# Keys of two attention layers laid in blocks of two heads, and their score products split into two halves of 32 rows

## The reference

```
q = rms_norm(x @ Wq + bq, gq).reshape(b, -1, n, d)
k_img = rms_norm(ctx_img @ Wk_img + bk_img, gk_img).reshape(b, -1, n, d)
v_img = (ctx_img @ Wv_img + bv_img).reshape(b, -1, n, d)
img_x = _attend(q, k_img, v_img)
out = (txt_x + img_x).reshape(b, -1, n * d)
return out @ Wo + bo
```

## Time and profile before

| | |
|---|---|
| Median of three runs | 3621.99 us (3617.33 to 3624.5) |
| The profiled execution | 3609.43 us, span 3607.7 us |
| Scatter stage with the keys and values | about 670 to 902 us of the span |
| Attention of layer 2 | about 2003 to 2205 us |
| Attention of layer 3 | about 2615 to 2816 us |

### The profile page before, as it was taken

One profiled execution on the slowest core, in us unless ns is written; L12 is line 12 of the kernel. 1 busy time (PEld: TensorE's weight loads), 2 busy tenths in 40 slices (PEclk: granted clock), 3 DMA queues, 4 the chain that ended last, 5 costly groups with the idle time before them and its releaser, 6 DMA issues. The chain is left out here.

```text
span 3607.7 us, 60300 instructions
## 1 busy us (share of the span) xinstructions
PE 2864.7 (79%) x20178; PEld 1832.3 (51%) x20178; DVE 2156.4 (60%) x4946; ACT 1479.5 (41%) x3032; POOL 1108.2 (31%) x1494
## 2 busy tenths in 40 slices
PE   5488886366899994589847798999889649999993
PEld 4233334122455553433323585444478648888882
DVE  7699994677677775634578686888777610000003
ACT  5377773254222224589835453222255211111120
POOL 3211110377233335412298441000044431111110
PEclk7599996698999997599969899999999669999996
DMA  8766643499422223688300440000044221112104
GB/s 272 195 114 119 120 105 140 151 371 356 138 80 82 77 82 132 166 136 137 59 1 1 160 145 27 1 1 1 1 160 133 96 60 56 47 53 79 60 29 140
DMA packets 261417, 386.10 MB, mean 107 GB/s; under 512 B 56673, under 2 KB 188750, under 8 KB 260864
## 3 DMA queue, kind: packets, MB, share of 16 engines
q1 hardware_dynamic: 230288, 305.68, 31.6%
q0 software_dynamic: 25152, 68.22, 5.4%
q10 hardware_dynamic: 5680, 8.39, 0.7%
HBM read 227.49 MB, written 160.24 MB: 107 GB/s over the span
## 5 line engine op out<-in xcount | busy, mean ns | idle before, releaser
L3172 POOL DMA_INDIRECT rows_out<-e_out,e_tr_dest x224 | 234.8, 1048 | 867.3 <-DVE e_out L3822 506.4
L3822 DVE COPY e_out<-e_psD 128x512 f32<-128x512 f32 x40 | 27.7, 692 | 495.4 <-PE e_psD L3790 495.2
L1243 ACT ACTIVATE a_pt<-a_psS 128x512 f32<-128x512 f32 x512 | 277.6, 595 | 107.9 <-PE a_psS L1139 103.5
L3584 PE MATMUL e_psG<-e_wgu,e_yT 128*128 x576 | 277.8, 605 | 29.3 <-ACT e_yT L3616 26.7
L1265 DVE TENSOR_REDUCE a_mx_sb<-a_psM 128x4 f32<-128x1024 f32 x256 | 293.2, 1215 | 12.3 <-PE a_psM L1122 11.4
L1153 PE MATMUL a_psV<-a_pt,a_vt 128*18 128x256 f32 x4096 | 291.2, 386 | 2.6 <-issue 2.1
L3790 PE MATMUL e_psD<-e_w,e_hT 128*128 128x256 f32 x1280 | 291.8, 388 | 0.0
L3779 PE MATMUL e_psH<-e_yT,e_w 128*128 128x256 f32 x1280 | 284.5, 381 | 1.6 <-issue 0.8
L3722 ACT ACTIVATE e_hT<-e_psH 128x512 f32<-128x512 f32 x160 | 95.5, 597 | 454.0 <-PE e_psH L3779 454.0
L3790 PEld LDWEIGHTS e_psD<-e_w,e_hT 128*128 128x128 f32 x1280 | 247.2, 196 | 33.7
L3779 PEld LDWEIGHTS e_psH<-e_yT,e_w 128*128 128x128 f32 x1280 | 244.2, 191 | 35.6 <-issue 2.1
(11 more groups left out here) (433 smaller groups left out, 6126.0 us busy)
## 6 DMA issues: line engine op xcount, KB each, us to landing
kbd<-e_wd SPq DMA_DIRECT2D x64, 512.0 KB, 3.8
cr_kbd<-kbd SPq DMA_DIRECT2D x64, 512.0 KB, 3.6
rows_in<-zeros POOLq DMA_DIRECT2D x36, 522.0 KB, 6.5
e_xin<-rows_in SPq DMA_DIRECT2D x144, 128.0 KB
vbd<-e_bd SPq DMA_DIRECT2D x64, 272.0 KB, 3.9
cr_vbd<-vbd SPq DMA_DIRECT2D x64, 272.0 KB, 2.7
cq_rows<-rows_out SPq DMA_DIRECT2D x32, 512.0 KB, 6.0
e_w<-in_L_ffn_w_dram SPq DMA_DIRECT2D x16, 1024.0 KB, 7.6
```

What stands on the lines that cost most here:

```text
L1243: act.activation(pt[:, probs(t, h), b, :, :], psS[:, unit(t, h, b) % S_BANKS, :].rearrange("p (k c) -> p k c", k=KC), ACT.Exp, scale=scale ...
L3172: pool.indirect_dma_start(out=self.rows_out[0:limit, :], out_offset=bass.IndirectOffsetOnAxis(ap=self.dest[:, t:t + 1], axis=0), in_=rows, ...
L3584: ins = pe.matmul(psG[:, u, :], yT[:, u, k, :], wgu[:, e, k, :], start=(k == 0), stop=(k == KC - 1))
```

## The change

CJ becomes 2. The keys are laid in blocks of two heads: 32 partitions with 128 columns, so an item is 128 partitions by 512 columns, 256 KB, in SBUF, in the store and in the load. The mask for it is cut in four parts of 32 partitions. A tile's scores become 16 products of 32 rows and 128 columns, in two halves j of eight: half 0 on the row groups 0 and 1, half 1 on the row groups 2 and 3. Both halves write to the same two PSUM banks, and the second waits for the last products of the first. In TensorE's step the first half stands where the scores stood, then come the turn of the input and the query projection, then the second half, then the turn of the probabilities. Semaphores of the scores become four.

```
-CJ = 4
+CJ = 2
+CR = CJ * CW
...
-        self.kbd = room_a[:, 12:16, :].rearrange("p (u x) c -> p u (x c)", u=2)
+        self.kbd = room_a[:, 12:14, :]
...
-        for half in range(2):
-            rows = self.mask[SEQ * half:SEQ * half + SEQ, :]
+        pool.wait_ge(self.made, 6)
+        for part in range(P // CR):
+            rows = self.mask[CR * part:CR * part + CR, :]
...
-    s_done = [core.sem(f"{n}sd{r}") for r in range(2)]
+    s_done = [core.sem(f"{n}sd{g}") for g in range(2 * CJ)]
...
-                def scores(t):
+                def scores(t, j):
                     u, m = t % 3, t % NK
-                    pe.wait_ge(q_ready, t + 1)
-                    pe.wait_ge(k_loaded[m], 16 * (t // NK + 1))
-                    if t:
-                        pe.wait_ge(shifted, t)
+                    if j == 0:
+                        pe.wait_ge(q_ready, t + 1)
+                        pe.wait_ge(k_loaded[m], 16 * (t // NK + 1))
+                        if t:
+                            pe.wait_ge(shifted, t)
+                    else:
+                        for r in range(2):
+                            pe.wait_ge(s_done[r], t + 1)
                     for k in range(KC):
                         for b in range(2):
                             for r in range(2):
-                                rows = slice(SEQ * r, SEQ * r + SEQ)
-                                ins = pe.matmul(psS[SEQ * b:SEQ * b + SEQ, r, k, :], qT[rows, u, k, SEQ * b:SEQ * b + SEQ],
-                                                kbd[rows, m, k, b, :], start=True, stop=True, tile_position=(SEQ * r, SEQ * b))
+                                g = 2 * j + r
+                                rows = slice(CR * g, CR * g + CR)
+                                ins = pe.matmul(psS[SEQ * b:SEQ * b + SEQ, r, k, j, :], qT[rows, u, k, SEQ * b:SEQ * b + SEQ],
+                                                kbd[rows, m, k, b, :], start=True, stop=True, tile_position=(CR * g, SEQ * b))
...
                     if ok(s + 1):
-                        scores(s + 1)
+                        scores(s + 1, 0)
                     if ok(s + 4):
                         turn_y(s + 4)
-                    if ok(s):
-                        turn_probs(s)
                     if ok(s + 3):
                         project(s + 3)
+                    elif ok(s):
+                        turn_probs(s)
+                    if ok(s + 1):
+                        scores(s + 1, 1)
+                    if ok(s) and ok(s + 3):
+                        turn_probs(s)
                     if ok(s - 1):
                         values(s - 1)
...
-                        for r in range(2):
-                            dve.wait_ge(s_done[r], t + 1)
+                        for g in range(2 * CJ):
+                            dve.wait_ge(s_done[g], t + 1)
```

More of the change, by code:

```diff
@@ L1452, in gpsimd_setup @@
                 pool.memset(v[SEQ * hh:SEQ * hh + SEQ, :, hh, CW], 1.0).then_inc(self.made, 1)
-        for half in range(2):
-            rows = self.mask[SEQ * half:SEQ * half + SEQ, :]
+        pool.wait_ge(self.made, 6)
+        for part in range(P // CR):
+            rows = self.mask[CR * part:CR * part + CR, :]
             pool.affine_select(out=rows, in_=rows, compare_op=ALU.is_ge, fill=0.0, base=0,
                                pattern=[[-CW, CJ]], channel_multiplier=1).then_inc(self.made, 1)
-        pool.wait_ge(self.made, 8)
-        for half in range(2):
-            rows = self.mask[SEQ * half:SEQ * half + SEQ, :]
+        pool.wait_ge(self.made, 10)
+        for part in range(P // CR):
+            rows = self.mask[CR * part:CR * part + CR, :]
             pool.affine_select(out=rows, in_=rows, compare_op=ALU.is_ge, fill=0.0, base=CW - 1,
                                pattern=[[CW, CJ]], channel_multiplier=-1).then_inc(self.made, 1)
-        pool.wait_ge(self.made, 10)
+        pool.wait_ge(self.made, 14)
     def gpsimd(self, pool, tile):
@@ L1503, in square @@
             act.activation(self.junk, self.kv[:, i % 4, 0:DIM], ACT.Square, accum_out=self.square[:, i:i + 1]).then_inc(self.squared, 1)
-        act.wait_ge(self.made, 10)
+        act.wait_ge(self.made, 14)
         for i in range(self.ITEMS):
@@ L1522, in vector_setup @@
         dve.tensor_tensor(self.gain, self.gain, self.query_gain, ALU.mult).then_inc(self.gained, 1)
-        dve.wait_ge(self.made, 10)
+        dve.wait_ge(self.made, 14)
         dve.wait_ge(self.gained, 1)
@@ L1622, in phase_cross @@
         psQ = ps(ctx, n + "psQ", [P, 2, DIM])
-        psS = ps(ctx, n + "psS", [P, 2, KC, CJ * SEQ])
+        psS = ps(ctx, n + "psS", [P, 2, KC, 2, CJ * SEQ])
         psP = ps(ctx, n + "psP", [P, 2, 4, P])
@@ L1647, in _ @@
                     if t >= NK:
-                        for r in range(2):
-                            sp.wait_ge(s_done[r], t - NK + 1)
+                        for g in range(2 * CJ):
+                            sp.wait_ge(s_done[g], t - NK + 1)
                     sp.dma_start(kbd[:, t % NK, :, :, :].rearrange("p k b c -> p (k b c)"), kbd_dram[t]).then_inc(k_loaded[t % NK], 16)
@@ L1732, in scores @@
                             for r in range(2):
-                                rows = slice(SEQ * r, SEQ * r + SEQ)
-                                ins = pe.matmul(psS[SEQ * b:SEQ * b + SEQ, r, k, :], qT[rows, u, k, SEQ * b:SEQ * b + SEQ],
-                                                kbd[rows, m, k, b, :], start=True, stop=True, tile_position=(SEQ * r, SEQ * b))
+                                g = 2 * j + r
+                                rows = slice(CR * g, CR * g + CR)
+                                ins = pe.matmul(psS[SEQ * b:SEQ * b + SEQ, r, k, j, :], qT[rows, u, k, SEQ * b:SEQ * b + SEQ],
+                                                kbd[rows, m, k, b, :], start=True, stop=True, tile_position=(CR * g, SEQ * b))
                                 if k == KC - 1 and b == 1:
-                                    ins.then_inc(s_done[r], 1)
+                                    ins.then_inc(s_done[g], 1)
                 def turn_probs(t):
@@ L1758, in values @@
                             for j in range(2):
-                                pair = 4 * k + 2 * r + j
+                                pair = 4 * k + 2 * j + r
                                 for b in range(2):
@@ L1859, in _ @@
                         t = s + 1
-                        for r in range(2):
-                            dve.wait_ge(s_done[r], t + 1)
-                        rows = psS[:, :, :, :].rearrange("p r k (j c) -> p (r k j) c", c=SEQ)
+                        for g in range(2 * CJ):
+                            dve.wait_ge(s_done[g], t + 1)
+                        rows = psS[:, :, :, :, :].rearrange("p r k j (h c) -> p (r k j h) c", c=SEQ)
                         dve.tensor_reduce(mx[:, :], rows, AX_X, ALU.max).then_inc(maxed, 1)
@@ L1872, in _ @@
                         if t >= 3:
-                            for r in range(2):
-                                dve.wait_ge(s_done[r], t - 2)
+                            for g in range(2 * CJ):
+                                dve.wait_ge(s_done[g], t - 2)
                             dve.wait_ge(q_squared, t - 2)
```

## The result

The changed kernel took 3697.03 us (median of 4 runs, 3692.48 to 3705.17) against 3623.24 for the kernel before on the same chip, a ratio of 1.0208 with a 95% interval of 1.0189 to 1.0227: 74 us slower, where 42 were forecast.

The account below looks back on a forecast made before the run. TensorE paced attention and POOL the scatter stage; a ring of waits would then pace attention. Two attention stages +48.4 and the scatter stage -6 gave +42 on 3622.0, so 3664 us, range 3636 to 3688.

Parts of the forecast that it names:

- Attention, the chain that becomes the pace: Attention stages: a ring of waits through TensorE, VectorE and ScalarE sets the step at 6.25 us, bounds 6.0 and 6.7.
- The ring that was named: Attention: turn, projection, half 1, maximum, subtraction, exponential, squares, copy of the sums, next turn; 6.24 us; chance 0.71.
- TensorE's own step: Attention: TensorE's own work per step grows from 5.67 to about 6.0 us, by 0.14 for halves and 0.20 for shape changes.
- the changes of shape: TensorE in attention: from scores on, four switches between product shapes become six, costing at most 0.20 us a step.
- The prediction's other reading: TensorE in attention: weight loads pulled ahead make shape changes free; step 5.8 us, whole gain over the sum about 6 us.
- The sum of a stage: Each attention stage: 22.8 us from first to last maximum plus 1.4 before it, 24.2 us longer; 48.4 for two.
- the first maximum: Start of an attention stage: VectorE's first maximum of scores comes 1.4 us later, behind half 0, turn, projection and half 1.
- The scatter stage: Key laying and storing beside POOL's scatters: 3 us gained in the middle and 3 at the end, -6, bounds -1 to -11.
- The mask's selects: POOL, scatter stage: four more selects lie hidden under its 11.2 us wait at the start; uncovered, they cost about 1 us.
- Rival 3: Scatter stage: memory is the pace, so fewer stored bytes save 48 us, meeting the attention's loss; 3622 us; chance 0.05.
- Rival 1: Attention: TensorE alone is the pace, the ring being shorter than 6.0 us; +22, 3644 us; chance 0.16.
- Rival 2: Attention: the halves don't run four abreast, TensorE's step 6.9 us; total +82, 3704 us; chance 0.08.

Follow-up runs that it names:

- the doubled store: Small key blocks placed into zeroed buffers with the attention of before, plus every key block stored a second time, against the kernel before: 3619.45 us, ratio 0.9997.
- the version that places small blocks: Changed kernel's scatter stage with the attention of before, four transfers placing each tile's keys into zeroed buffers, against the kernel before: 3605.3 us, ratio 0.9956.

## Why the prediction was wrong

- **The step that failed** is "Attention, the chain that becomes the pace". It followed one ring through VectorE and ScalarE and took it for the longest, with "bounds 6.0 ... and 6.7, if a half takes as long as all scores do now". The measured 6.69 is at that bound by chance: a half takes 0.59. The part named the work that waits behind the maximum on ScalarE, but not the addition of the bias that is queued behind it on VectorE and on which TensorE's output projection waits. From half 1 on that ring is 0.89 to the maximum, 2.40 to the addition (2156.72 to 2159.12), 0.48 to the output projection, 1.06 to half 0, 0.59, 0.17 and 1.09: 6.68. All of it but some 0.07 between the end of the addition and the load stands in the trace of before or in the sum, and the wait stands in the code. That trace has the same ring without turn, projection and half 1, with about half a microsecond to spare (the 0.55 above); the change puts them into it, and the prediction did not follow that line.
- **The ring that was named** is real: 6.24 was worked out, 6.29 measured once the other was opened, with the forecast idle of 0.25 before the turn. It only was not the longest.
- **TensorE's own step**: 6.0 against 5.99. The halves cost 0.17 instead of 0.14, the changes of shape some 0.15 instead of 0.20. The Trainium skill's "TensorEngine Tiling (Array Packing)", section "Tiling Modes", by which a change of mode empties the array, agrees with the row: a half streams for some 0.44, by the estimate of the prediction, and takes 0.59. The prediction's other reading, that loads pulled ahead would make the changes cost nothing, is not borne out, since the step would be 5.8.
- **The sum of a stage** was 24.2 and became 44.0 in layer 2 (first load of the stage to that of the next: 203.4 to 247.4) and 43.5 in layer 3. In layer 2 the 24 steps from the fifth on give 10.6 of the missing 19.8 (160.6 against 24 x 6.25), the first four 4.7 (29.7 against 25), the first maximum 1.8 (+3.2 against +1.4), the last three steps 1.5 and the end 1.3. The second error is the clock that the sum took for the filling. The first three of these steps, 7.83, 7.81 and 7.73, run at mean granted clocks of 0.68, 0.50 and 0.72; the fourth, at 1.00, takes 6.33, near the 6.25 of the sum, although half 0 still comes right behind the subtraction there. With the same order and 64-row products it was likewise 7.82 in the first such step and 6.28 in the fourth, at 1.00.
- **The scatter stage**: -6 forecast; from first scatter to the experts' load -6.3 in the profiled execution and some -10 over all traces, inside the bounds. The mask's selects take 1.0 of that back: they stand ahead of the first scatter, and the forecast had them hidden under a later wait. And I gave part of the gain to the layings; the doubled store shows that it is the bytes. Rival 3 was half right on the cause: the stores do hold the stage up in places, for 6 to 10 us and not for 48. That POOL's own row sets the rest was argued from its sum and not tested.
- **Rival 1** (TensorE alone, 3644) is what is left when the three rings are open: 5.99 us a step and 3645.89. **Rival 2** (3704) came nearest in time but its mechanism is refuted by the half's 0.59 us.
- The stages of the traces add up to 87.5 - 6.3 + 1.0 = 82 us, the medians to 74 (68 to 82 by the interval); I leave the difference at that. Likewise the version that places small blocks gains 18 us by the medians. In the profiles 8.7 are in the scatter stage and 3.3 in the two attention stages, from first load to that of the next stage (203.4 to 201.3 and 202.4 to 201.2); where the rest is, no trace here shows.

## What to carry to other kernels

When an operation moves later on the engine that sets the pace, follow every engine that waits for it, and on each list all that is queued behind the waiting instruction up to the next thing that the pacing engine waits for: each such line is a ring, and the longest counts. Here there were three within half a microsecond (6.69, 6.29 and 6.23 us), and opening one showed the next. A wait that was met with half a microsecond to spare before the change is where to look first. A smaller layout in memory need not be the layout that the products use: transfers can place small blocks into buffers that were zeroed once, and the order of the pacing engine stays as it was.

## What was not expected of the hardware

- A half that waits for the end of TensorE's own half just ahead came 0.84 us behind it from load to load, against 0.59 for the turn, which does not wait for it; no other engine is in between.
- Four transfers of 64 KB in place of one of 512 KB per tile cost the attention nothing that shows.
